# A fused retention and FP4 feed-forward kernel: the set-up reordered, the end written out

## The chip, the cores and the metric

The kernel runs on one NeuronCore of a Trainium2 chip. The metric is the device time of one launch in microseconds, the median of three runs. PE is the matrix engine (TensorE), DVE the vector engine, ACT the scalar engine, POOL GpSimd; SP issues nearly all DMAs. Each engine works through its own instruction list in order, and semaphores are the only thing that ties the lists together.

## The reference

The input x is 8 sequences of 1024 rows of 256 numbers. What is computed, cut to what matters:

```python
xn = layernorm(x)                                   # over the last axis, no gain
# branch 1: retention with 8 heads of 32
Q, K = rotate_and_scale(xn @ W_Q), rotate_and_scale(xn @ W_K, downscale=True)
V = xn @ W_V
scores = (Q @ K^T) * decay_mask                     # causal, gamma_h ** (n - m)
Y = per_head_layernorm(scores @ V) * gn_weight + gn_bias
a = (silu(xn @ W_G) * Y) @ W_O
# branch 2: feed-forward on blockwise FP4 numbers (blocks of 16, scale = max|.|/6)
q = fp4_quant_dequant
h = silu(q(xn) @ q(w_gate)^T) * (q(xn) @ q(w_up)^T)   # 704 wide
f = q(h) @ q(w_down)^T
out = x + a + f
```

## The kernel before

The 8192 rows are 64 tiles of 128 rows (t = 0 to 63; 8 tiles make a sequence). The retention is computed by chunks: within a tile by scores, across tiles by a running 32x32 state for each head, which starts anew with each sequence.

All five engines run a software pipeline that is unrolled in Python. `step(i)` of an engine holds the pieces of several tiles that it does in that step: i+2 (the statistics), i+1 (normalising and quantising x), i (projections, gate and up, rotation, scores), i-1 (values, group norm, quantising h), i-2 (down projection, z), i-3 (the last two matmuls and the residual). So i runs from FIRST = -4 to LAST = 66; steps -2 and -1 fill the pipeline, steps 64 to 66 empty it. The order within a step is written out by hand and is the same in all steps; the pieces that don't exist are skipped.

Products of float32 accuracy are made of three matmuls (`product`, L897 to L900): each operand is split into a high and a low part. A high part is an ACT copy to fp32r, the low part the difference. In step i PE does the product of x with the Q and K columns (`b_qk`, L913), the two transposes of the quantised x (L931), work of older tiles, gate and up in three products (L898 to L900, `gu_c`, `gu_b`, `gu_a`), the V and gate columns (`vg`) and the scores (L1085). The residual (DVE L591) adds x to `b_out` and lets SP store the tile.

The weights are prepared on the chip during the first steps, by pieces that are inserted where `i == -2`, `-1`, `0` or `1`:

- The 1408 gate and up rows come in three parts (n = 0, 1, 2), the down weights in two (n = 3, 4). Each part is quantised: `largest`, `invert`, `divide` (DVE; POOL does `divide` of 3 and 4, L520), `size` (POOL L515, the scale), `magnitude` (ACT L816), `round_off` (DVE, three passes L558, L561, L565; the third waits for `size`).
- Each part is two groups m = 2n, 2n+1. `turn` (PE) transposes a group, `high_part` (ACT L829) copies it, `turn_rest` (PE) forms the remainder in PSUM and `low_part` (ACT L835) copies it; for groups 4 and 5 the low part is DVE's `low_difference`. `double` and `clear_low_half` handle the last 64 rows of the down weights.
- The projection weights `w_qkvg` are two halves, Q and K (c = 0), V and gate (c = 1). `total_qkvg(c)` (ACT L847, four instructions with an accumulator) sums the rows, `mean_qkvg(c)` (POOL L502) scales, `centre_qkvg` subtracts the mean: for c = 0 ACT does it (L854), for c = 1 POOL (L508). Then `turn_qkvg`, `qkvg_high_part` (L861), `turn_qkvg_rest`, `qkvg_low_part` (L868), for m = 0, 1 (c = 0) and m = 2, 3 (c = 1).

In the steps that empty the pipeline, PE keeps the step's order: in step 64 the transposes of z and of h of tile 62 stand before the state and value matmuls of tile 63, and in step 65 the transposes of z of tile 63 (L941, which wait for z) stand before all that is left of tile 63's feed-forward:

```python
pe.wait_ge(z_ready, t + 1)                    # step(i), t = i - 2
... z transposes, h transposes (L946, L950), first down matmuls (L989), rest of them
```

On DVE the sum of squares of tile t (L656) comes after the h remainders of tile t-1 and the first rounding pass (L644) of tile t.

## Time and profile before

| | us |
|---|---|
| median of 3 runs | 898.14 (897.17 to 898.86) |
| the profiled execution, its own time | 897.34 |
| its span in the trace | 895.5 |
| PE busy | 861.6 (96%) |
| DVE busy | 839.4 (94%) |
| POOL busy | 678.7 (76%) |
| ACT busy | 444.5 (50%) |

The span is the time from the first to the last event of the profiled execution; 1.84 us of its own time lie outside it. Busy time is the sum of an engine's instructions, overlaps counted once.

### The profile page before, as it was taken

What the parts mean: (1) busy time and instruction counts of PE and PEld (TensorE: products, weight loads), DVE (VectorE), ACT (ScalarE), POOL (GpSimd) and SP (SyncE); (2) the same over time, 40 slices, a digit from 0 to 9 for tenths busy, and PEclk for the clock granted to TensorE, in tenths of its full rate; (3) what the DMA queues carried; (4) which work ended last, traced back from release to release, by engine and by line L of the source; (5) the groups of instructions that cost most, each with busy time, mean ns of one, the idle gap of its engine ahead of it and who ended that gap; (6) DMA issues with size and microseconds to landing.
All of it is one profiled execution on the core that took longest, in us unless ns stands there. A gap on an engine that the chain in (4) does not pass through costs nothing.

```text
span 895.5 us, 21445 instructions
## 1 busy us (share of the span) xinstructions
PE 861.6 (96%) x8370; PEld 747.2 (83%) x8370; DVE 839.4 (94%) x1883; ACT 444.5 (50%) x1146; POOL 678.7 (76%) x794
## 2 busy tenths in 40 slices
PE   2789999999999999999999999999999999999996
PEld 1668888888888888888888888888888888888885
DVE  7879999999999999999999999999999999999985
ACT  5654454545445454454554445454454544545442
POOL 4767777778778777877877777787787778778774
PEclk9999999999999999999999999999999999999999
DMA  9200110110111011011101101101110110110000
GB/s 322 92 1 19 37 37 19 37 37 24 32 37 33 23 37 37 19 36 37 31 26 36 37 19 37 37 24 31 37 36 20 37 38 18 37 37 13 7 13 18
DMA packets 30052, 33.68 MB, mean 38 GB/s; under 512 B 3328, under 2 KB 28672, under 8 KB 29696
## 3 DMA queue, kind: packets, MB, share of 16 engines
q1 hardware_dynamic: 29808, 32.26, 11.5%
q8 instruction: 66, 1.08, 0.5%
q14 instruction: 34, 0.28, 0.1%
q10 hardware_dynamic: 144, 0.07, 0.0%
HBM read 23.92 MB, written 8.39 MB: 36 GB/s over the span
## 4 chain that ended last, share of the span: by engine, by line
PE 93%; POOL 2%; DVE 2%; ACT 1%; DMA 1%; issue 1%; SPq 0%; POOLq 0%; DVEq 0%
PE quad L900 12%; PE quad L898 12%; PE quad L899 12%; PE quad L1085 5%; PE bank L898 5%; PE quad L966 4%; PE quad L989 4%; PE bank L900 3%; PE bank L899 3%; PE bank L1022 3%; PE quad L1069 3%; PE quad L990 3%; PE quad L946 2%; PE quad L950 2%; PE quad L958 2%; PE quad L1074 2%
## 5 line engine op out<-in xcount | busy, mean ns | idle before, releaser
L898 PE MATMUL quad<-w_gu_hi,xqT_hi 128*128 128x512 f32 (+1 forms) x384 | 149.5, 389 | 1.9 <-DVE xqT_lo L600 1.9
L900 PE MATMUL quad<-w_gu_hi,xqT_lo 128*128 128x512 f32 (+1 forms) x384 | 143.8, 375 | 0.0
L899 PE MATMUL quad<-w_gu_lo,xqT_hi 128*128 128x512 f32 (+1 forms) x384 | 142.5, 371 | 0.0
L467 POOL TENSOR_TENSOR rstd<-var_eps,power 128x9 f32<-128x9 f32 x67 | 124.1, 1852 | 5.6
L456 POOL TENSOR_TENSOR x_quot<-xn,x_inv 128x256 f32<-128x256 f32 x64 | 40.4, 631 | 89.8 <-DVE x_inv L648 89.8
L442 POOL TENSOR_TENSOR h_quot<-h,h_inv 128x704 f32<-128x704 f32 x64 | 88.9, 1390 | 5.1
L475 POOL TENSOR_TENSOR xT_lo<-xT_in,xT_hi 128x256 fp32r<-128x256 f32 x64 | 47.4, 740 | 59.9 <-ACT xT_hi L797 59.9
L452 POOL TENSOR_TENSOR qk<-qk_cos,qk_sin 128x512 f32<-128x512 f32 x64 | 82.9, 1295 | 5.8 <-PE bank L976 0.8
L495 POOL TENSOR_TENSOR gate_gn<-gate,gn 128x512 f32<-128x512 f32 x64 | 82.9, 1296 | 0.0
L900 PEld LDWEIGHTS quad<-w_gu_hi,xqT_lo 128*128 128x128 f32 x384 | 72.0, 188 | 11.4
L898 PEld LDWEIGHTS quad<-w_gu_hi,xqT_hi 128*128 128x128 f32 x384 | 72.5, 189 | 9.7 <-issue 2.0
L899 PEld LDWEIGHTS quad<-w_gu_lo,xqT_hi 128*128 128x128 f32 x384 | 72.7, 189 | 8.5
L807 ACT ACTIVATE xn<-x_in,x_shift,rstd 128x256 f32<-128x256 f32 x64 | 38.5, 602 | 78.8 <-POOL x_shift L479 78.8
L658 DVE SCALAR_TENSOR_TENSOR h_grid<-h_magic,h_diff 128x704 f16<-128x704 bf16 x64 | 76.7, 1198 | 0.0
L729 ACT ACTIVATE xqT_hi<-bank 128x256 fp32r<-128x256 f32 x64 | 24.6, 385 | 97.6 <-PE bank L931 97.6
L465 POOL TENSOR_SCALAR var_eps<-moments 128x9 f32<-128x9 f32 x67 | 60.3, 899 | 7.6 <-DVE moments L656 4.3
L713 DVE TENSOR_TENSOR probs<-quad,causal 128x512 f32<-128x512 f32 x64 | 44.2, 690 | 22.9 <-PE quad L1085 22.2
L778 ACT ACTIVATE silu<-quad 128x512 f32<-128x512 f32 x64 | 38.3, 599 | 51.1 <-PE quad L900 51.1
L761 ACT ACTIVATE x_magic<-x_quot 128x256 bf16<-128x256 f32 x64 | 26.7, 417 | 71.7 <-POOL x_quot L456 71.7
L752 ACT ACTIVATE y_sq<-bank 128x256 f32<-128x256 f32 x64 | 24.6, 384 | 75.1 <-PE bank L1016 75.1
L668 DVE TENSOR_TENSOR hq<-h_grid,h_scale 128x704 f32<-128x704 f16 x64 | 57.8, 904 | 0.1
L898 PE MATMUL bank<-w_qkvg_hi,xT_hi 128*128 128x512 f32 x128 | 57.2, 447 | 0.3 <-POOL xT_lo L475 0.3
(176 smaller groups left out, 2893.2 us busy)
## 6 DMA issues: line engine op xcount, KB each, us to landing
x_in<-in_x_dram SPq DMA_DIRECT2D x64, 128.0 KB, 2.2
xT_in<-in_xT_dram SPq DMA_DIRECT2D x64, 128.0 KB, 2.2
out_dram<-y_out SPq DMA_DIRECT2D x64, 128.0 KB, 1.7
sin<-const_sin_dram SPq DMA_DIRECT2D x1, 1792.0 KB, 11.4
raw<-in_w_gu_dram SPq DMA_DIRECT2D x2, 512.0 KB, 7.2
w_qkvg<-in_w_qkvg_dram SPq DMA_DIRECT2D x1, 1024.0 KB, 8.3
cos<-const_cos_dram SPq DMA_DIRECT2D x1, 896.0 KB, 7.2
raw<-in_w_down_dram SPq DMA_DIRECT2D x2, 352.0 KB, 8.7
```

The lines of the kernel that those rows point to most:

```text
L442: pool.tensor_tensor(blocks(h_quot[:]), blocks(h[:]), spread(h_inv[:]), ALU.mult).then_inc(h_divided, 1)
L452: pool.tensor_tensor(qk[:], qk_cos[:], qk_sin[:], ALU.add).then_inc(rope_add, 1)
L465: pool.tensor_scalar(var_eps[:], moments[:, 1:], EPS, None, ALU.add).then_inc(var_ready, 1)
L467: pool.tensor_tensor(rstd[:, (t + 3) % RING, 0:1 + H], var_eps[:], power[:], ALU.pow).then_inc(rstd_ready, 1)
L475: pool.tensor_tensor(xT_lo[:], xT_in[:, t % SLOTS], xT_hi[:].bitcast(F32), ALU.subtract).then_inc(x_low, 1)
L495: pool.tensor_tensor(gate_gn[:, t % 2, :, :], gate[:].unsqueeze(1).broadcast_to([P, 2, D]), gn[:], ALU.mult).then_inc(gate_scaled, 1)
L658: dve.scalar_tensor_tensor(h_grid[:], h_magic[:], LEAST, h_diff[:], ALU.max, ALU.subtract).then_inc(h_gridded, 1)
L668: dve.tensor_tensor(blocks(hq[:, 0:F]), blocks(h_grid[:]), spread(h_scale[:]), ALU.mult).then_inc(h_quant, 1)
L898: pe.matmul(out, hi[:, k], w_hi[:, k], start=start, stop=False)
L899: pe.matmul(out, hi[:, k], w_lo[:, k], start=False, stop=False)
L900: return pe.matmul(out, lo[:, k], w_hi[:, k], start=False, stop=stop)
L1085: ins = pe.matmul(quad[:, r, g * P:(g + 1) * P], kT[rows, g, :], qT[rows, g, :], start=True, stop=True)
```

## The change

Nothing in the arithmetic changes, and steps 2 to 63 stay as they are but for two leftover pieces of set-up in ACT's step 2. The first part of the diff moves set-up pieces, the second replaces steps 64 to 66 of DVE, ACT and PE by a function `drain()` each, with an order of its own. POOL keeps its steps up to 66. SP is untouched. The core of the diff, condensed to one line for each inserted call, by engine:

```diff
 POOL
 step(-1), before the wait for x_peak:
+    mean_qkvg(0)
 step(0), after the rotation's add (L452):
+    size(4); divide(4)
 step(-1), after x_quot (L456):
-    mean_qkvg(0)
+    size(1); size(2)
 step(-1), after x_shift (L479):
-    size(1)
     mean_qkvg(1); centre_qkvg()
 between step(-1) and step(0):
-    size(2)
     size(3); divide(3)
-    size(4); divide(4)

 DVE
 step(0), after qk_cos (L603):
+    largest(4); invert(4)
     low_difference(4, 5)
 step(1), after qk_cos:
+    round_off(4)
 step(0), before the product with silu (L684):
-    round_off(4)
 step(-1), at its end:
     round_off(1); round_off(2); largest(3); invert(3)
-    largest(4); invert(4)

 ACT
 step(-1), before x_magic (L761):
     magnitude(0)
+    total_qkvg(0)
     high_part(0, 1)
+    centre_qkvg()
     magnitude(1)
-    total_qkvg(0)
 step(-1), before xn (L807):
-    centre_qkvg()
+    qkvg_high_part(0, 1)
     low_part(0, 1)
+    qkvg_low_part(0, 1)
     total_qkvg(1)
+    magnitude(2)
 step(-1), after xn:
-    magnitude(2); qkvg_high_part(0, 1); qkvg_low_part(0, 1)
 between step(-1) and step(0):
     high_part(2, 3)
-    qkvg_high_part(2); low_part(2, 3)
 step(0), after xqT_hi (L729):
+    low_part(2, 3)
     high_part(4, 5)
+    qkvg_high_part(2)
+    magnitude(3)
     qkvg_low_part(2)
-    magnitude(3)
     out_high_parts()
 step(0), before x_magic:              + qkvg_high_part(3)
 step(0), after x_magic:                 magnitude(4)    - qkvg_high_part(3)
 step(0), before gate (L790):            double(3)       - double(4)
 step(0), high_part(6, 7): moved from before xT_hi (L797) to after it
 step(1): high_part(8), low_part(8), high_part(9), low_part(9), clear_low_half()
     stood before xqT_hi, before yT, before kT, and (the last two) before silu;
     now high_part(8) before x_magic, double(4) before silu, low_part(8) after silu,
     high_part(9) before xT_hi, and in step(2), before xqT_hi:
+    low_part(9); clear_low_half()

 PE
 step(0), before the Q and K product:
-    turn(2, 3)
 step(0), after the Q and K product:
-    turn_qkvg(2)
+    turn(2, 3)
 step(0), after the x transposes:
     turn_rest(2, 3); turn(4, 5)
+    turn_qkvg(2)
     turn_qkvg_rest(2)
 step(1): turn(8), turn_rest(8), turn(9), turn_rest(9) stood before and after the
     Q and K product, before gu_c and after the qk transposes; now after gu_b,
     after gu_a, after vg and after the scores

 DVE, ACT and PE, at the end
-for i in range(LAST + 1):
+for i in range(TILES):
     step(i)
+drain()
```

The order of the new `drain()` functions, with t = 63:

```python
# PE: zT_lo matmuls (61) | z transposes (62) | state matmuls (63) | value matmuls (63)
#     | h transposes (62) | y transposes (63) | down_first, down_rest, project_out (62)
pe.wait_ge(h_twice, t + 1)
turn_h(t)
down_first(t)
turn_z(t)
down_rest(t)
project_out(t)
# DVE: masked0 (63), h_inv (63), z low (62), residual(61), h low 0 (62),
#      sum of squares (63), h low 1 (62), h_diff, h_grid, hq (63), y_part (63),
#      residual(62), h low 0, h low 1, z low, residual (63)
# ACT: z high (62), yT (63), h high 0 (62), y_sq (63), h high 1 (62), h_magic (63),
#      last 64 columns of hq (63), h high 0, h high 1, z high (63)
```

The new PE functions issue the same matmuls as the step did. `down_first(t)` waits for the first high part of h and for the residual of tile t-1, then does 6 matmuls; `down_rest(t)` does 11 in the order high part 1, low part 1, low part 0, each behind its wait; `project_out(t)` does 4 with z's high part and 2 with its low part.

## Rows read from the trace of the kernel before

**Rows 1.** The page's chain that ended last, shares of the span by engine.

```profile
PE 93%; POOL 2%; DVE 2%; ACT 1%; DMA 1%; issue 1%; SPq 0%; POOLq 0%; DVEq 0%
```

**Rows 2.** Windows: start:end, length, busy us of each engine, granted PE clock, DMA.

```profile
75.50:858.00 782.50, 782.50 (x7730) 680.62 (x7724) 753.90 (x1723) 390.54 (x1014) 610.04 (x717) 1.00 0.10 30
...
884.00:895.50 11.50, 5.50 (x31) 4.96 (x31) 2.70 (x7) 1.43 (x4) 2.80 (x3) 0.85 0.07 23
```

**Rows 3.** Timeline, set-up, ACT: start, duration, instruction, [idle before, releaser].

```profile
12.65 0.49 ACT L829 ACTIVATE w_gu_hi<-quad 128x384 fp32r<-128x384 f32 x1 [4.03 <-PE quad L1111]
...
14.63 0.41 ACT L847 ACTIVATE w_qkvg<-w_qkvg 128x256 f32<-128x256 f32 x1
...
16.84 1.69 ACT L854 ACTIVATE w_qkvg<-w_qkvg,w_mean 128x256 f32<-128x256 f32 x4
...
41.70 0.60 ACT L868 ACTIVATE w_qkvg_lo<-quad 128x512 fp32r<-128x512 f32 x1 [0.67 <-PE quad L1158]
```

**Rows 4.** SP's issue of the projection weights, and its time to landing.

```profile
3.06 0.43 SPq L401 DMA_DIRECT2D w_qkvg<-in_w_qkvg_dram  x1
...
w_qkvg<-in_w_qkvg_dram SPq DMA_DIRECT2D x1, 1024.0 KB, 8.3
```

**Rows 5.** Timeline, set-up, PE.

```profile
24.08 1.12 PE L1152 MATMUL quad<-ident,w_qkvg 128*128 128x128 f32 x4 [3.53 <-ACT w_qkvg_hi L861]
...
27.71 0.47 PE L898 MATMUL bank<-w_qkvg_hi,xT_hi 128*128 128x512 f32 x1
...
45.45 0.73 PE L1085 MATMUL quad<-qT,kT 32*128 32x128 f32 x16 [0.36 <-ACT val L791]
...
56.02 0.33 PE L1125 MATMUL quad<-ident,raw 128*128 128x128 f32 x1 [1.60 <-ACT w_dn_hi L829]
...
61.70 0.73 PE L1085 MATMUL quad<-qT,kT 32*128 32x128 f32 x16 [1.02 <-ACT val L791]
62.72 0.50 PE L898 MATMUL bank<-w_qkvg_hi,xT_hi 128*128 128x512 f32 x1 [0.29 <-POOL xT_lo L475]
```

**Rows 6.** Timeline, set-up, DVE.

```profile
25.00 1.30 DVE L561 SCALAR_TENSOR_TENSOR w_magic<-w_magic,raw 128x1024 f16<-128x1024 bf16 x1
29.52 1.23 DVE L565 TENSOR_TENSOR raw<-w_magic,w_scale 128x1024 f32<-128x1024 f16 x1 [3.22 <-POOL w_scale L515]
...
32.13 0.88 DVE L540 TENSOR_REDUCE w_max<-raw 128x44 f32<-128x704 f32 x1
```

**Rows 7.** Timeline, set-up, POOL.

```profile
22.56 0.23 POOL L502 TENSOR_SCALAR w_mean<-w_sum 128x4 f32<-128x4 f32 x1
22.89 6.00 POOL L508 TENSOR_SCALAR w_qkvg<-w_qkvg,w_mean 128x256 f32<-128x256 f32 x4
28.97 0.44 POOL L515 TENSOR_SCALAR w_scale<-w_max 128x64 f32<-128x64 f32 x1
...
37.68 1.20 POOL L456 TENSOR_TENSOR x_quot<-xn,x_inv 128x256 f32<-128x256 f32 x1 [0.36 <-DVE x_inv L648]
```

**Rows 8.** Timeline, the end, PE.

```profile
878.64 0.45 PE L958 MATMUL quad<-qT,state 32*32 32x128 f32 x16
...
887.47 0.69 PE L941 MATMUL bank<-ident,z 128*128 128x128 f32 x2 [4.65 <-POOL z L489]
...
892.57 0.40 PE L923 MATMUL quad<-w_out_hi,zT_lo 128*128 128x256 f32 x2
```

**Rows 9.** Timeline, the end, DVE.

```profile
881.64 0.41 DVE L656 TENSOR_REDUCE moments<-y_sq 128x8 f32<-128x256 f32 x1
...
882.88 0.89 DVE L668 TENSOR_TENSOR hq<-h_grid,h_scale 128x704 f32<-128x704 f16 x1
...
893.00 0.42 DVE L591 TENSOR_TENSOR y_out<-quad,x_in 128x256 f32<-128x256 f32 x1 [1.46 <-PE quad L923]
```

**Rows 10.** Timeline, the end, POOL.

```profile
883.05 2.41 POOL L467 TENSOR_TENSOR rstd<-var_eps,power 128x9 f32<-128x9 f32 x1
...
886.69 0.72 POOL L489 TENSOR_TENSOR z<-y_part,gate_gn 128x256 f32<-128x256 f32 x1 [0.54 <-DVE y_part L705]
```

More of the change, by code:

```diff
@@ L452, in step @@
                     pool.tensor_tensor(qk[:], qk_cos[:], qk_sin[:], ALU.add).then_inc(rope_add, 1)
+                    if i == 0:
+                        size(4)
+                        divide(4)
                 if exists(i + 1):
@@ L527, in _ @@
                 step(i)
-            size(2)
             size(3)
             divide(3)
-            size(4)
-            divide(4)
             for i in range(LAST + 1):
@@ L605, in step @@
                     if i == 0:
+                        largest(4)
+                        invert(4)
                         low_difference(4, 5)
+                    if i == 1:
+                        round_off(4)
                 if exists(i + 2):
@@ L695, in step @@
                         invert(3)
-                        largest(4)
-                        invert(4)
                 if exists(i):
@@ L725, in step @@
                     t = i
-                    if i == 1:
-                        high_part(8)
+                    if i == 2:
+                        low_part(9)
+                        clear_low_half()
                     act.wait_ge(x_turned, t + 1)
@@ L889, in _ @@
             high_part(2, 3)
-            qkvg_high_part(2)
-            low_part(2, 3)
-            for i in range(LAST + 1):
+            for i in range(TILES):
                 step(i)
+            drain()
         @block.tensor
@@ L1051, in step @@
                     ins.then_inc(vg_ready, 1)
+                    if i == 1:
+                        turn(9)
                     if i == 0:
@@ new lines, in down_first, with down_rest @@
+            def down_first(t):
+                pe.wait_ge(hT_high0, t + 1)
+                pe.wait_ge(summed, t)
+                for k in range(3):
+                    pe.matmul(b_out, hT_hi[:, k], w_dn_hi[:, k], start=k == 0, stop=False)
+                    ins = pe.matmul(b_out, hT_hi[:, k], w_dn_lo[:, k], start=False, stop=False)
+                ins.then_inc(down_h0, 1)
+            def down_rest(t):
+                pe.wait_ge(hT_high1, t + 1)
+                for k in range(3, 5):
+                    pe.matmul(b_out, hT_hi[:, k], w_dn_hi[:, k], start=False, stop=False)
+                    ins = pe.matmul(b_out, hT_hi[:, k], w_dn_lo[:, k], start=False, stop=False)
+                ins.then_inc(down_h1, 1)
+                pe.wait_ge(hT_low1, t + 1)
+                for k in range(3, 5):
+                    pe.matmul(b_out, hT_lo[:, k], w_dn_hi[:, k], start=False, stop=False)
+                pe.matmul(b_out, hT_hi[:, 5], w_dn_hi[:, 5], start=False, stop=False)
+                pe.matmul(b_out, hT_hi[:, 5], w_dn_lo[:, 5], start=False, stop=False).then_inc(down_l1, 1)
+                pe.wait_ge(hT_low0, t + 1)
+                for k in range(3):
+                    ins = pe.matmul(b_out, hT_lo[:, k], w_dn_hi[:, k], start=False, stop=False)
+                ins.then_inc(down_l0, 1)
@@ new lines, in project_out @@
+            def project_out(t):
+                pe.wait_ge(z_high, t + 1)
+                for k in range(KD):
+                    pe.matmul(b_out, zT_hi[:, k], w_out_hi[:, k], start=False, stop=False)
+                    ins = pe.matmul(b_out, zT_hi[:, k], w_out_lo[:, k], start=False, stop=False)
+                ins.then_inc(out_high, 1)
+                pe.wait_ge(z_low, t + 1)
+                for k in range(KD):
+                    ins = pe.matmul(b_out, zT_lo[:, k], w_out_hi[:, k], start=False, stop=k == KD - 1)
+                ins.then_inc(out_ready, 1)
@@ new lines, in drain @@
+            def drain():
+                t = TILES - 1
+                for k in range(KD):
+                    ins = pe.matmul(b_out, zT_lo[:, k], w_out_hi[:, k], start=False, stop=k == KD - 1)
+                ins.then_inc(out_ready, 1)
+                turn_z(t - 1)
+                pe.wait_ge(masked1, t + 1)
+                for g in range(G):
+                    for r in range(HG):
+                        rows = place(g, r)
+                        ins = pe.matmul(b_yT[g][quarter(r), :], state[rows, g * HD:(g + 1) * HD], qT[rows, g, :], start=True, stop=False)
+                ins.then_inc(st_ready, 1)
+                pe.wait_ge(masked0, t + 1)
+                for g in range(G):
+                    for r in range(HG):
+                        head = (g * HG + r) * HD
+                        ins = pe.matmul(b_yT[g][quarter(r), :], val[:, head:head + HD], probs[:, (r + g) % HG, g * P:(g + 1) * P],
+                                        start=False, stop=True)
+                ins.then_inc(yT_ready, 1)
+                turn_h(t - 1)
+                pe.wait_ge(yT_copy, t + 1)
+                pe.wait_ge(z_low, t)
+                for g in range(G):
+                    ins = pe.transpose(b_y[:, g * P:(g + 1) * P], yT[:, g * P:(g + 1) * P], ident[:])
+                ins.then_inc(y_ready, 1)
+                down_first(t - 1)
+                down_rest(t - 1)
+                project_out(t - 1)
+                pe.wait_ge(h_twice, t + 1)
+                turn_h(t)
[3 more added lines that the diff above has]
+                project_out(t)
@@ L1168, in _ @@
             turn_qkvg_rest(0, 1)
-            for i in range(LAST + 1):
+            for i in range(TILES):
                 step(i)
+            drain()
 AHEAD = 7
```

122 lines of the change are left out of this document (98 added, 24 removed).

## The prediction, made before the changed kernel was run

> **What bounds the kernel now.** I read the page's chain of waits first: 93% of it is PE [rows 1]. Then the windows: from 75.5 to 858 us PE is busy in every microsecond, at the full granted clock [rows 2], DVE in 753.90 of 782.50. The change leaves that stretch alone, so it passes through as it is, and only its ends can move. Its length is 61 to 62 tiles of some 13.1 us, from the scores of tile 1 at 61.70 [rows 5] on. What precedes 61.70, and what follows the last tile's scores, is set by waits; there I went through the timeline engine by engine. A landmark that comes d us earlier at the front is d us at the end, as long as PE stays the bound between.
>
> **The front: the first projection.** ACT now sums the columns before the first high parts. The weights are issued at 3.06 and land 8.3 us later, at 11.4 [rows 4]; four sums at 0.40 us each (14.63 to 16.23 before, [rows 3]) end at 13.0. The high part that was ready at 12.65 so starts 0.35 us late, a loss that I count: it is what the transposes behind it wait for. The centring stood at 16.84 and took 1.69 us [rows 3]; now it runs at 13.8 to 15.5, directly behind the high parts. PE's transposes of these weights start near 15.7. Their high parts no longer stand behind the second half's sums, xn and magnitude(2), but behind magnitude(1), x_magic and xT_hi (1.05 + 0.4 + 0.4, to 17.0), so the remainder group that started at 24.08 can start at 17.6, 6.5 us earlier. It took 3.6 us from there to the Q and K product at 27.71 [rows 5]; the product comes at 21.2. This large shift is not the gain, since what it needs next is elsewhere: PE goes on to wait for the second weight part.
>
> **The front: DVE and POOL.** DVE stood 3.22 us before its third rounding pass because POOL gave the scale of part 2 only at 28.97, behind its 6.00 us of centring [rows 6, 7]. Now POOL makes both scales near 15.3 to 16.3. What is late next is magnitude(2): ACT does it after the sums of the second half, 21.15 + 1.6 + 1.0 = 23.75. Part 2 is then rounded in 3.75 us, to 27.55; before, to 30.75 (29.52 + 1.23, [rows 6]). DVE also loses largest(4) and invert(4) there (0.88, [rows 6], plus 0.65 for the two small ones) and comes to the work of step 0 some 4.5 us earlier, at 29.1. They come back behind qk_cos.
>
> POOL is the engine that does not get earlier. Its centring needs the sums of the second half, which ACT now ends at 22.75 instead of 20.8; mean and start of centring are 22.8 and 23.15, against 22.56 and 22.89 [rows 7]. The four instructions took 6.00 us. The first took 2.79 of it and the last two 0.92 each, once DVE was idle, so the work alone is 3.7 us and the rest is time lost beside DVE's rounding. In the 3.4 us in which DVE was busy beside it (to 26.30, [rows 6]), about 1.1 us of work got done. With the same rate beside the 3.75 us of rounding part 2, the centring ends at 29.6. From below 28.0 (a full 3.7 us of work plus 1.2 lost), from above 30.5. From 29.6 POOL does, without a wait: size(3), divide(3), x_scale, the rotation's add, size(4), divide(4), by 35.1, and x_quot of tile 1 in 1.20 us, as at 37.68 [rows 7], since DVE is in the same rounding pass then. It ends at 36.3 against 38.88, 2.6 us earlier.
>
> The Trainium skill, SBUF — State Buffer, section "Who interferes with whom", says that a DVE instruction with two SBUF inputs and a GpSimd instruction that reads SBUF exclude each other for a whole instruction. The stretched 2.79 us in the trace agree in kind. By the strict rule the second centring instruction would wait out all the rounding: 27.55 + 2.8 = 30.35, so 0.75 us less gain.
>
> **The front: steps 0 and 1.** Behind x_quot stand on ACT x_magic, magnitude(4), the two copies of k and q, and the last low part of the projection weights, which ran at 41.70 [rows 3] and now ends at 38.6 instead of 42.3. PE has finished its third gate-up product by then (at 38.3) and starts the V and gate columns at 38.65. The scores of tile 0, waiting for val, start at 40.9 against 45.45 [rows 5]: 4.5 us earlier. Now xT_hi of tile 1 goes ahead of the high parts 6 and 7, so POOL's xT_lo no longer holds the next product up, and turn(8), which stood in front of it, is gone from there: the Q and K product of tile 1 comes at 43.05, not 48.17, 5.1 us earlier. In step 1 PE lost 1.60 us to the high part of group 9 [rows 5]; its transposes now stand behind vg, at the price of a wait of about 0.3 us for the low part of group 8, and round_off(4), three passes of 0.9, is on DVE before h_diff. I find the scores of tile 1 at 56.05 (61.70 before). The last remainder, group 9, then stands between the scores and the next product, and high_part(9) ahead of xT_hi: tile 2's product at 57.4 against 62.72 [rows 5]. The front gains **5.2 us**. Its bounds: 3.3 if the centring and ACT's chain are each a microsecond later than drawn and step 1's last insertions cost their full 0.8 us of PE; 6.4 if the centring ends at 28.0.
>
> **The end** (in the times of before, without the front's shift). Before, the state matmuls of tile 63 start at 878.64, behind six transposes of h of tile 62 that wait for the masked scores [rows 8]. Now they come first, some 1.2 us earlier, the y transposes and y_sq 1.0 us earlier, and on DVE the sum of squares stands ahead of h_diff: it starts at 880.05, not 881.64 [rows 9], 1.6 us earlier. POOL's eps and power (2.41, [rows 10]) and all behind it move with it, so z is ready at 885.8, not 887.4. The quantised h of tile 63 (882.88 + 0.89, [rows 9]) stays where it was, for h_magic is behind one more copy.
>
> Before, PE sat idle for 4.65 us until z, and had then everything of tile 63 to do: 5.5 us from 887.47 to the end of the last matmul (892.57 + 0.40, [rows 8]). Now the h transposes run at 884.2, down_first at 885.4 (it waits for the residual of tile 62, 885.35), and z's transposes at 886.1; left are 17 matmuls 0.12 us apart and the last one's 0.16: 888.55. The old last matmul ended at 892.97, so the gain is 4.4. This holds at the full clock. In the last window of before the granted clock is 0.85 [rows 2], so part of it ran at the lower of its levels, 1.2 GHz, right behind the 4.65 us of idleness. The new order leaves PE idle for only 1.35 us (882.85 to 884.2). If the clock falls anyway, the first 12 instructions take 1.0 us longer and the gain is 3.4. I take 4.2; the bounds are 2.9 and 4.8.
>
> The Trainium skill, TensorE: Matmul & The Clock Gate, section "What's actually happening", says that an idle array runs at half clock until activity releases it. The trace agrees where the idleness was 4.65 us; whether 1.35 us is enough for it no row here shows.
>
> **Sum.** 5.2 + 4.2 = 9.4 us off 897.34, the profiled execution's own time: 887.9. The median of the runs is 0.8 above that execution: 888.7.
>
> **Rivals.**
> 1. *POOL's centring is stretched further* and carries the whole of step 0. For it: 2.79 us for a 0.92 us instruction, beside the very kind of pass that will run beside it now. Against it: two of four ran free. It gives a front gain of 3.3 and the same end: 890.6. Chance 0.17.
> 2. *The clock falls in the short gap, and the end gains only its first part.* For it: the 0.85 of [rows 2]. Against: the gap is under a third of the old one. 888.7 + 1.2 = 889.9. Chance 0.17.
> 3. *The front gain is given back in step 2*, because the last low part and clear_low_half (0.8 us of ACT) now stand ahead of xqT_hi, and ACT's early arrival is eaten by a DVE that is behind; only the end counts: 898.14 - 4.2 = 893.9. Against it: ACT is idle half of the time. Chance 0.04.
> 4. *Slower.* The steady stretch settles into another phase of DVE against POOL, in which their shared passes collide more. DVE has (782.50 - 753.90) / 60 = 0.48 us to spare for each tile [rows 2]; beyond that it sets the pace. It decides from 0.48 + 9.4 / 61 = 0.63 us of added stretch for each tile; at 0.7 us the kernel takes 888.7 + 61 x 0.22 = 902. For it: DVE's passes do get stretched. Against: PE's own order sets the phase and is unchanged. Chance 0.03.
> 5. *The moves do nothing at the front*, the total being set by a landing. Against it: DMA is idle in the stretch from 30 us on, and every landing needed precedes that. The end alone, as in 3: 893.9. Chance 0.03.
>
> **How the numbers follow.** The forecast has 0.56. A measurement can tell 0.2%, 1.8 us. Faster needs under 896.3, which all cases but the fourth and a remnant give: 0.94; within 0.2%, 0.03; slower, 0.03. Bounds of both terms, 3.3 + 2.9 and 6.4 + 4.8, give 892.0 and 886.9, and a run's median may lie 0.7 to either side: the range is 886.2 to 892.7.
>
> **What would show it.** Right: column sums starting at 11.4; the Q and K product of tile 0 near 21; no wait of DVE for the scale, but a short one for magnitude(2); centring ending at 29 to 30; scores of tiles 0 and 1 at 41 and 56; PE without idle time until the end; from the last state matmuls to the last residual's start 11.2 us (877.4 to 888.6) instead of 14.4 (878.64 to 893.00). Wrong: idle PE in step 2 or later, centring past 31, or z's transposes later than 887.

## The result, and the profile of the changed kernel

| | before | after |
|---|---|---|
| median of the runs | 898.34 us (897.17 to 898.86, 5 runs, the three of the earlier table among them) | 888.18 us (887.87 to 889.64, 5 runs) |
| profiled execution | 897.34 us, span 895.5 | 888.04 us, span 886.2 |

The ratio is 0.9895 [0.9881, 0.9908]. The forecast was 888.7 for the median and 9.4 us off the profiled execution's time; that one moved by 897.34 - 888.04 = 9.30 us. The five runs of the changed kernel lie in two groups, 887.87, 888.04, 888.18 and 889.41, 889.64; that comes back below.

First the chain of waits of the changed kernel: PE's share is what it was in [rows 1], and POOL's has gone from 2% to 1% while DVE's rose from 2% to 4%.

```profile
PE 93%; DVE 4%; POOL 1%; DMA 1%; issue 0%; ACT 0%; SPq 0%; POOLq 0%
```

Windows of the changed kernel, in the columns of [rows 2]. The long stretch is PE's alone as before. The last stretch is the first difference: its granted clock is 1.00, where [rows 2] had 0.85.

```profile
50.00:53.00 3.00, 3.00 (x16) 2.41 (x16) 3.00 (x9) 1.17 (x4) 1.49 (x2) 1.00 0.02 5
70.00:852.00 782.00, 782.00 (x7727) 680.27 (x7727) 753.35 (x1723) 389.54 (x1011) 609.35 (x717) 1.00 0.10 30
878.00:886.20 8.20, 4.10 (x31) 3.66 (x31) 3.76 (x8) 1.51 (x4) 0.94 (x2) 1.00 0.09 32
```

The set-up, PE. The landmarks of [rows 5] have moved: the remainder group 24.08 to 17.55, the Q and K product of tile 0 27.71 to 20.99, the scores of tile 0 45.45 to 40.62, the product of tile 1 48.17 to 42.39, the scores of tile 1 61.70 to 56.28, the product of tile 2 62.72 to 57.57. Among the waits that are left are 1.07 us for DVE's rounding, 0.59 for the centring, and in step 1 a new one of 1.69 for POOL's qk.

```profile
17.55 0.66 PE L1316 MATMUL quad<-ident,w_qkvg 128*128 128x128 f32 x4 [0.45 <-ACT w_qkvg_hi L943]
...
20.99 0.47 PE L979 MATMUL bank<-w_qkvg_hi,xT_hi 128*128 128x512 f32 x1 [1.86 <-POOL xT_lo L481]
...
27.21 0.66 PE L1275 MATMUL quad<-ident,raw 128*128 128x128 f32 x4 [1.07 <-DVE raw L567]
...
28.90 0.71 PE L1303 MATMUL quad<-by_head,w_qkvg 128*128 128x128 f32 x4 [0.59 <-POOL w_qkvg L513]
...
40.62 0.73 PE L1163 MATMUL quad<-qT,kT 32*128 32x128 f32 x16 [0.36 <-ACT val L844]
...
42.39 0.40 PE L979 MATMUL bank<-w_qkvg_hi,xT_hi 128*128 128x512 f32 x1
...
49.31 0.66 PE L1096 MATMUL bank<-ident,qk 128*128 128x128 f32 x4 [1.69 <-POOL qk L454]
...
56.28 0.73 PE L1163 MATMUL quad<-qT,kT 32*128 32x128 f32 x16 [0.80 <-ACT val L844]
...
57.57 0.50 PE L979 MATMUL bank<-w_qkvg_hi,xT_hi 128*128 128x512 f32 x1
```

ACT in the set-up, against [rows 3]: the column sums begin as soon as the weights land, and the centring follows the first high parts directly.

```profile
10.41 0.42 ACT L929 ACTIVATE w_qkvg<-w_qkvg 128x256 f32<-128x256 f32 x1 [1.71 <-DMA w_qkvg<-in_w_qkvg_dram]
...
12.74 0.49 ACT L911 ACTIVATE w_gu_hi<-quad 128x384 fp32r<-128x384 f32 x1 [0.62 <-PE quad L1275]
...
13.77 1.69 ACT L936 ACTIVATE w_qkvg<-w_qkvg,w_mean 128x256 f32<-128x256 f32 x4
```

DVE in the set-up, against [rows 6]: the third rounding pass of part 1 stands at 21.96, that of part 2, which had 3.22 us of waiting, at 25.77, both without a wait, and part 2 is rounded at 25.77 + 1.38 = 27.15. The last two rows are one pass of the same size: 0.89 us in step 0, 1.83 in step 1.

```profile
21.96 1.22 DVE L567 TENSOR_TENSOR raw<-w_magic,w_scale 128x1024 f32<-128x1024 f16 x1
...
25.77 1.38 DVE L567 TENSOR_TENSOR raw<-w_magic,w_scale 128x1024 f32<-128x1024 f16 x1
...
36.51 0.89 DVE L567 TENSOR_TENSOR raw<-w_magic,w_scale 128x704 f32<-128x704 f16 x1
...
48.17 1.83 DVE L567 TENSOR_TENSOR raw<-w_magic,w_scale 128x704 f32<-128x704 f16 x1
```

POOL in the set-up, against [rows 7]: the centring ends at 23.38 + 5.47 = 28.85, x_quot of tile 1 at 35.72 instead of 38.88. No row has a wait, and several durations are long: POOL works without a break and is stretched.

```profile
16.80 2.74 POOL L473 TENSOR_TENSOR rstd<-var_eps,power 128x9 f32<-128x9 f32 x1
...
22.02 1.26 POOL L507 TENSOR_SCALAR w_mean<-w_sum 128x4 f32<-128x4 f32 x1
23.38 5.47 POOL L513 TENSOR_SCALAR w_qkvg<-w_qkvg,w_mean 128x256 f32<-128x256 f32 x4
...
34.52 1.20 POOL L461 TENSOR_TENSOR x_quot<-xn,x_inv 128x256 f32<-128x256 f32 x1
...
46.44 0.91 POOL L448 TENSOR_SCALAR x_scale<-x_max 128x16 f32<-128x16 f32 x1
47.43 1.83 POOL L454 TENSOR_TENSOR qk<-qk_cos,qk_sin 128x512 f32<-128x512 f32 x1
```

The end, PE, against [rows 8], from the scores of tile 63. The idle stretch is 1.42 us where it was 4.65, it stands ahead of the transposes of h and no longer ahead of those of z, and these are now surrounded by work.

```profile
870.53 0.73 PE L1163 MATMUL quad<-qT,kT 32*128 32x128 f32 x16
...
872.07 0.45 PE L1229 MATMUL quad<-qT,state 32*32 32x128 f32 x16 [0.16 <-DVE probs L715]
...
879.31 0.55 PE L1178 MATMUL quad<-ident,hq 128*128 128x128 f32 x3 [1.42 <-ACT hq L891]
...
880.44 0.39 PE L1188 MATMUL quad<-w_dn_hi,hT_hi 128*128 128x256 f32 x1 [0.25 <-ACT hT_hi L873]
...
881.25 0.38 PE L1173 MATMUL bank<-ident,z 128*128 128x128 f32 x2
```

DVE in the end, against [rows 9]: the sum of squares, the quantised h, the last residual.

```profile
874.83 0.41 DVE L748 TENSOR_REDUCE moments<-y_sq 128x8 f32<-128x256 f32 x1
...
877.78 1.19 DVE L755 TENSOR_TENSOR hq<-h_grid,h_scale 128x704 f32<-128x704 f16 x1
...
883.70 0.42 DVE L720 TENSOR_TENSOR y_out<-quad,x_in 128x256 f32<-128x256 f32 x1 [1.19 <-PE quad L1216]
```

POOL in the end, against [rows 10]: the power starts at 875.66 and takes 1.83 us, not 2.41, and then z.

```profile
879.38 0.72 POOL L494 TENSOR_TENSOR z<-y_part,gate_gn 128x256 f32<-128x256 f32 x1 [1.16 <-DVE y_part L757]
```

I measure each end of the kernel from one landmark, the scores of tile 63. PE's row of them in the kernel before:

```profile
875.70 0.73 PE L1085 MATMUL quad<-qT,kT 32*128 32x128 f32 x16
```

They were at 875.70 and are at 870.53, so the front gave 5.17 us. From them to the start of the last residual it was 893.00 - 875.70 = 17.30 us and is 883.70 - 870.53 = 13.17: the end gave 4.13.

### The profile page after: what moved, and what is told of

Read it like the earlier page. It is cut to its first block, busy times and chain, and to the rows that moved or that the text cites. A ratio compares the mean times of both kernels' runs of the same rounds, so it can differ in the third digit from the quotient of the medians.

```text
span 886.2 us, 21445 instructions
## 1 busy us (share of the span) xinstructions
PE 859.9 (97%) x8370; PEld 744.5 (84%) x8370; DVE 840.4 (95%) x1883; ACT 443.7 (50%) x1146; POOL 679.7 (77%) x794
## 4 chain that ended last, share of the span: by engine, by line
PE 93%; DVE 4%; POOL 1%; DMA 1%; issue 0%; ACT 0%; SPq 0%; POOLq 0%
PE quad L981 12%; PE quad L979 12%; PE quad L980 12%; PE bank L979 5%; PE quad L1163 5%; PE quad L1042 4%; PE quad L1065 4%; PE bank L981 3%; PE bank L980 3%; PE bank L1096 3%; PE quad L1147 3%; PE quad L1066 2%; PE quad L1034 2%; PE quad L1022 2%; PE quad L1026 2%; PE quad L1152 2%
## 5 line engine op out<-in xcount | busy, mean ns | idle before, releaser
L981 PEld LDWEIGHTS quad<-w_gu_hi,xqT_lo 128*128 128x128 f32 x384 | 72.0, 188 | 11.4
```

The lines of the kernel that those rows point to most:

```text
L981: return pe.matmul(out, lo[:, k], w_hi[:, k], start=False, stop=stop)
```

## The experiments

Each is compared with the kernel before, run beside it on the same chip: its median was 897.75 for e1 to e4, 897.85 for e5 to e8, 899.12 for e9 to e12. The number in a label is that of its running order. A profile shows one run of each kernel; for e2, e3, e6, e7, e8 and e9 that was the longest one. The diffs are against the changed kernel where nothing else is said.

**The two ends by themselves (e1, e2).** One kernel has the new set-up and the old end (loops to LAST + 1, no drain), the other the old set-up and the new end.

```diff
# e1_front, on DVE, ACT and PE
-            for i in range(TILES):
+            for i in range(LAST + 1):
                 step(i)
-            drain()
# e2_end: the kernel before, with the new loops and drain() of all engines
```

> The set-up of the changed kernel with the old steps 64 to 66 at the end. Theory A (the two ends are separate and add): span shorter than before by what the scores of tile 63 moved, 5.2 us, so 893.1 us for the median; PE idle 4.65 us before z's transposes, granted clock below 1 behind it. Rival B (the front's gain is given back in the steady stretch, the end brought nearly all): 897 to 898.

Measured: 892.2 us (892.0 to 892.47), 5.55 below its before; ratio 0.9937 [0.9922, 0.9951]. The scores of tile 0 are at 40.43, of tile 1 at 56.12. (The projection weights landed 8.6 us after their issue here, not 7.3, ACT's sums began at 11.62 and the first high part behind them at 13.24, half a microsecond later than in the changed kernel, and yet these scores are not later; the rest of the set-up started 0.19 us earlier here.) Its last stretch is that of the kernel before, with the same 4.65 us and the fallen clock. First PE's row of it, then the window.

```profile
882.15 0.69 PE L1015 MATMUL bank<-ident,z 128*128 128x128 f32 x2 [4.65 <-POOL z L494]
```

```profile
880.00:890.20 10.20, 5.46 (x31) 4.92 (x31) 2.70 (x7) 1.37 (x3) 1.47 (x3) 0.83 0.08 26
```

> The old set-up with the new end alone. Theory A: 4.1 us off the median of before, 894.2; scores of tile 1 at 61.7 as before; last residual 13.2 us after the first scores of tile 63. Rival B: 889 to 890, nearly the whole gain.

Measured: 893.24 (893.07 to 894.02), 4.5 below; ratio 0.995 [0.9935, 0.9964]. From the scores of tile 63 (876.51) to the last residual (889.68) it is 13.17 us, exactly as in the changed kernel, and the clock is 1.00 from 880 us on. (In this profile everything starts 0.84 us later, the first high part at 13.49 for 12.65 in [rows 3], hence 876.51 and not 875.70.) 5.55 + 4.5 = 10.05, and both together measured 898.34 - 888.18 = 10.16. The ends add. Nothing of the front is given back in the long stretch.

**The sums back behind the high parts (e3).**

```diff
                         magnitude(0)
-                        total_qkvg(0)
                         high_part(0, 1)
+                        total_qkvg(0)
                         centre_qkvg()
```

> The changed kernel with ACT's first column sums put back behind the first high parts; the centring still stands right behind them. Theory A (POOL's centring of the second half carries step 0, and it starts when ACT has summed the second half): sums end at 15.4 instead of 12.1, ACT's chain is 1.9 to 2.1 us later, so POOL's centring starts 1.5 to 2 us later and the scores of tile 0 at 42.2 to 42.6 (40.6 in the changed kernel): 1.5 to 2.0 us slower than the changed kernel, 889.8. Rival C (the chain has slack there, since the first product waits 1.9 us for POOL's low part of x, not for the weights): less than 0.4 us lost.

Measured: 889.98 (889.33 to 890.01), ratio 0.991 [0.9895, 0.9925]. The product is at 23.14 instead of 20.99, 2.15 us later, the scores of tile 0 at 42.55 and of tile 1 at 58.23, 1.9 us later each. This one swap carries 1.9 of the front's 5.2 us. The size is theory A's, but not its carrier: POOL's centring ends 1.5 us later, at 30.36, and POOL then waits for DVE three times (0.29 us for the inverse of the weights, 0.22 for qk_cos, 0.15 for x_inv), while DVE itself had waited 1.43 us for ACT's magnitude(2).

**The transposes of the second part back ahead of the projection (e4, e9).**

```diff
+                    if i == 0:
+                        turn(2, 3)
                     if t == 0:
...
-                    if i == 0:
-                        turn(2, 3)
```

> The changed kernel with PE's transposes of the second part put back ahead of the first Q and K product. Theory A (DVE reads that product only at 28.9, PE idles before the third part's transposes): the product starts near 24.2 instead of 21.0 and nothing behind 28 us moves, scores of tile 0 at 40.6, no difference in time. Rival D (what the product delays on PE, the transposes of x and the remainders of the second part, comes 1.4 us later and carries on): 0.5 to 1.4 us slower.

Measured: 889.24 (888.79 to 889.81), ratio 0.9905 [0.9888, 0.9921]; the scores of tile 0 at 41.59, 1.0 us late, those of tile 1 at 57.27. The loss has the size that rival D expected, but not its cause. PE's rows of this kernel: after the idle 4.12 us the transposes take 1.11 us (0.66 in the changed kernel) and the products stand 0.43 us apart and not 0.23.

```profile
23.18 1.11 PE L1275 MATMUL quad<-ident,raw 128*128 128x128 f32 x4 [4.12 <-DVE raw L567]
...
24.80 0.78 PE L979 MATMUL bank<-w_qkvg_hi,xT_hi 128*128 128x512 f32 x1
```

The window over them gives the reason, a granted clock of 0.50, the lower of the two levels.

```profile
23.00:28.50 5.50, 5.33 (x19) 4.64 (x20) 5.36 (x8) 1.53 (x3) 5.40 (x5) 0.50 0.57 204
```

To part the order from the clock, the same order once more with 34 transposes of the identity into a free bank, to keep PE busy in the gap.

```diff
# on top of e4_turn
                     if i == 0:
+                        for k in range(34):
+                            pe.transpose(bank[1][:, 0:P], ident[:], ident[:])
                         turn(2, 3)
```

> The kernel e4_turn (second part's transposes back ahead of the first Q and K product) with 34 needless transposes of the identity put into PE's 4.1 us of idleness ahead of them; nothing else is changed. Theory K (e4_turn is a microsecond slower only because the granted clock fell to 0.50 behind that idleness): the clock stays 1.00 from 23 to 28.5 us, the product's six matmuls stand 0.23 us apart, scores of tile 0 at 40.6 to 40.8, time 888.0 to 888.3, as the changed kernel. Rival D (the order itself costs it, the transposes of x come behind the product): scores of tile 0 stay at 41.4 or later, 889 or more.

Measured: 889.24 (888.02 to 891.52), ratio 0.9898 [0.9879, 0.9917]. By the times theory K is not borne out: the median is that of e4, and one run of four lies in the 888.0 to 888.3 that it asked for. The profile, which is of the longest run, parts the two. The product starts late, but runs at the upper clock, and the scores of tile 0 are at 40.68, as in the changed kernel (40.62): up to there the whole microsecond was the clock, and the order itself costs nothing.

```profile
24.16 0.48 PE L979 MATMUL bank<-w_qkvg_hi,xT_hi 128*128 128x512 f32 x1
```

Its windows show where this run lost its time. From 50 us on, in step 1, where nothing differs from the changed kernel, the clock was 0.50, and the scores of tile 1 came at 57.94, 1.7 us late. It was 0.72 in the end too, from 880 to 886, with the same drain.

```profile
23.00:28.50 5.50, 5.07 (x34) 4.21 (x34) 5.38 (x6) 3.18 (x7) 5.40 (x5) 1.00 0.61 196
50.00:53.00 3.00, 3.00 (x10) 2.31 (x9) 2.94 (x8) 0.00 (x0) 1.42 (x2) 0.50 0.00 0
```

PE's rows of that end: the same 1.42 us of idleness as in the changed kernel, the first transposes and matmul as fast as there, and then the matmuls 0.21 us apart. From the scores of tile 63 (872.22) to the last residual (886.90) it is 14.68 us, 1.5 more than in the changed kernel's profile.

```profile
881.00 0.55 PE L1180 MATMUL quad<-ident,hq 128*128 128x128 f32 x3 [1.42 <-ACT hq L891]
...
882.68 0.41 PE L1191 MATMUL quad<-w_dn_lo,hT_hi 128*128 128x256 f32 x1
882.89 0.41 PE L1190 MATMUL quad<-w_dn_hi,hT_hi 128*128 128x256 f32 x1
```

**Who carries step 0, POOL or DVE (e5).** ACT, idle there, takes two of POOL's four centrings.

```diff
-                for j in range(4, 8):
+                for j in range(6, 8):
...
+            def centre_second():
+                act.wait_ge(qkvg_mean, 2)
+                for j in range(4, 6):
+                    act.activation(w_qkvg[:, j, :], w_qkvg[:, j, :], ACT.Identity, bias=w_mean[:, j:j + 1],
+                                   scale=1.0).then_inc(qkvg_centred[1], 1)
```

> The changed kernel with two of POOL's four centring instructions of the second half given to ACT (behind xn, before the second part's high parts). Forecast's theory P (POOL's centring carries step 0): it ends at 26 to 26.5 instead of 28.85, x_quot of tile 1 at about 32.5 instead of 34.52 and the scores of tile 0 1 us or more earlier. Rival theory V (DVE's own list carries it, with no idle time from 19 to 34.5 us; POOL merely arrives at the same time): x_quot moves only by what POOL's stretching of DVE's rounding costs, 0 to 0.4 us, and the scores of tile 0 by 0 to 0.4; time 887.8 to 888.2.

Measured: 887.5 (887.4 to 889.0), ratio 0.9888 [0.9872, 0.9905]. POOL's rows of this kernel: the centring is over at 26.38, 2.5 us earlier, and POOL then waits 1.51 us for DVE's largest.

```profile
23.23 3.15 POOL L513 TENSOR_SCALAR w_qkvg<-w_qkvg,w_mean 128x256 f32<-128x256 f32 x2
27.89 0.39 POOL L520 TENSOR_SCALAR w_scale<-w_max 128x44 f32<-128x44 f32 x1 [1.51 <-DVE w_max L542]
...
33.90 1.20 POOL L461 TENSOR_TENSOR x_quot<-xn,x_inv 128x256 f32<-128x256 f32 x1
```

x_quot ends at 35.10 (35.72), the scores of tile 0 are at 40.00 (40.62), of tile 1 at 55.68 (56.28). So 2.5 us less on POOL is worth 0.6 us at most: 0.15 of it is there before the change acts (the Q and K product at 20.84 for 20.99), and the other 0.46 is one small instruction of DVE, the second w_inv, which took 0.65 us beside POOL's rotation add and takes 0.19 now. That is nearer to theory V (0 to 0.4) than to P (1 us or more): DVE carries step 0, and POOL's part in it is what it stretches on DVE. My prediction had named POOL the carrier.

**Step 1: two passes of the last rounding moved out of it (e6),** to the end of step 0, where DVE was idle. `round_first` holds the first two of the three passes, `round_last` the third.

```diff
                     if i == 1:
-                        round_off(4)
+                        round_last(4)
...
+                    if t == 0:
+                        round_first(4)
```

> The changed kernel with the first two passes of DVE's rounding of part 4 moved from step 1 to the end of step 0, where DVE stands idle for 1.48 us; the third pass stays. Theory R (in step 1 the rounding stretches POOL's x_scale and rotation add, 0.91 and 1.83 us instead of 0.27 and 1.28, and PE waits 1.69 us for it): PE's wait falls to 0.3 to 0.8, scores of tile 1 at 55.0 to 55.5 (56.28 in the changed kernel), 887.1 to 887.5. Rival T (POOL is late because h_quot starts late, and DVE is busy anyway): the wait stays above 1.3 and the time at 888.2 or, since the two passes delay x_max, up to 0.5 slower.

Measured: 890.26 (889.32 to 890.75), ratio 0.9912 [0.9898, 0.9927], and the scores of tile 1 at 59.05, 2.8 us late. Both theories fall. The 1.69 us for qk did go, but only because PE comes later still: POOL's add now takes 1.27 us and not 1.83, and ends at 50.82, where it had ended at 49.26. DVE's rows show what took the place of that wait: beside POOL's gate_gn and the low part of the output weights the two passes take 1.89 and 1.84 us, not 0.87 and 0.89, x_max starts at 45.80 and not 43.64, and PE waits 2.67 us for probs, with a granted clock of 0.50 from 47 to 53 behind it. What the late passes and what the clock cost of the 2.8 us is not parted by a run. DVE's rows, then POOL's add:

```profile
42.11 1.89 DVE L573 SCALAR_TENSOR_TENSOR raw<-w_magic,raw 128x704 f32<-128x704 bf16 x1
44.03 1.84 DVE L576 SCALAR_TENSOR_TENSOR w_magic<-w_magic,raw 128x704 f16<-128x704 bf16 x1
45.80 0.41 DVE L596 TENSOR_REDUCE x_max<-xn 128x16 f32<-128x256 f32 x1
```

```profile
49.55 1.27 POOL L454 TENSOR_TENSOR qk<-qk_cos,qk_sin 128x512 f32<-128x512 f32 x1
```

**The sum of squares back behind h_diff (e7),** as in the kernel before, the rest of the drain left.

```diff
-                dve.wait_ge(squared, t + 1)
-                dve.tensor_reduce(moments[:, 2:], ...)
                 h_low_part1(t - 1)
                 dve.wait_ge(h_abs, t + 1)
                 dve.scalar_tensor_tensor(h_diff[:], ...)
+                dve.wait_ge(squared, t + 1)
+                dve.tensor_reduce(moments[:, 2:], ...)
```

> The changed kernel with the sum of squares of the last tile put back behind h_diff in the written-out end. Forecast's theory Z (z's path sets the end, 1.6 us of its gain come from this move): z's transposes and the last residual 1.2 us later, 889.4. Rival H (the end now hangs on the quantised h: its transposes, high part and first down matmuls; z has 1.1 us to spare): less than 0.5 us, z's transposes at most 0.3 later, 888.2 to 888.7.

Measured: 892.13 (891.25 to 893.66), ratio 0.9936 [0.9921, 0.9951]; from the scores of tile 63 to the last residual 17.26 us and not 13.17. Both expectations are far too small. The profile is of the longest of the four runs and had lost 1.5 us in step 1 as well; by the medians the move back costs 892.13 - 888.18 = 3.95 us, by the fastest runs 3.4. PE's rows, then DVE's:

```profile
880.62 0.55 PE L1178 MATMUL quad<-ident,hq 128*128 128x128 f32 x3 [1.34 <-ACT hq L891]
...
883.60 0.55 PE L1188 MATMUL quad<-w_dn_hi,hT_hi 128*128 128x256 f32 x1 [2.10 <-DVE y_out L720]
```

```profile
882.70 0.42 DVE L757 TENSOR_TENSOR y_part<-bank,y_gain 128x256 f32<-128x256 f32 x1 [2.42 <-POOL y_gain L477]
883.04 0.41 DVE L720 TENSOR_TENSOR y_out<-quad,x_in 128x256 f32<-128x256 f32 x1
```

The down product accumulates where the residual of tile 62 has to be read first, and that residual stands on DVE behind y_part, which waits 2.42 us for POOL's gain. So all of PE's last work waits for z's path, not only the transposes of z. It starts 11.58 us behind the scores of tile 63 and not 9.91, which is 1.67 of the 4.1 us. The other 2.4 come behind it: the matmuls stand 0.21 us apart, 0.12 in the changed kernel, at a granted clock of 0.71 from 880 to 891.8.

**What the clock is worth in the old end (e8):** the kernel before, with 36 transposes of the identity ahead of its wait for z.

```diff
# against the kernel before
                     t = i - 2
+                    if i == TILES + 1:
+                        for k in range(36):
+                            pe.transpose(bank[1][:, 0:P], ident[:], ident[:])
                     pe.wait_ge(z_ready, t + 1)
```

> The kernel before, with 36 needless transposes of the identity into an unused bank put into PE's 4.65 us of idleness ahead of the last tile's z transposes; nothing else is changed. Theory K (the lower clock behind the idleness costs over 1 us): the granted clock stays 1.00 in the last 11 us, the last six h transposes take 0.49 instead of 0.85 for three, last residual 1.0 to 1.3 us after less time: 896.5 to 896.9 against 897.8. Rival L (the ACT copies between set the pace): less than 0.4 us.

Measured: 896.53 (896.29 to 899.39, 10 runs), 1.3 below its before by the medians; ratio 0.9991 [0.9982, 1.0001], which leaves the total open. Three of the ten runs are 1.7 us or more above the median, and the profile is of the longest. Its scores of tile 1 are at 63.64 and not 61.70, 1.6 us of that lost in step 1 with a granted clock of 0.57 from 56 to 60 us, and 3.57 us lie between the start of the last residual and the end of the span, for 2.50. The end between these is clearer, 16.47 us from the scores of tile 63 to the last residual instead of 17.30, with a granted clock of 1.00 in the stretch of the gap (0.87 in the kernel before). The 0.83 us gained lie between theory K (1.0 to 1.3) and rival L (under 0.4), nearer to K.

```profile
56.00:60.00 4.00, 3.65 (x11) 2.97 (x12) 1.96 (x5) 1.65 (x6) 2.91 (x3) 0.57 0.00 0
...
880.00:890.00 10.00, 9.28 (x105) 8.48 (x104) 5.21 (x11) 2.77 (x7) 5.90 (x5) 1.00 0.07 24
```

**The two groups of runs (e10).** Two runs of the changed kernel are 1.5 us longer; their mean granted clock is 0.998 against 1.000. The falls seen in the kernel with filled order, whose mean is 0.996, are candidates, 1.5 to 1.7 us each. Ahead of the one in step 1 PE is idle for 1.69 us, so 12 transposes of the identity were put there.

```diff
                     t = i
+                    if i == 1:
+                        for k in range(12):
+                            pe.transpose(bank[6][:, 0:P], ident[:], ident[:])
                     pe.wait_ge(rope_add, t + 1)
```

> The changed kernel with 12 needless transposes of the identity into an unused bank, put ahead of PE's wait for the rotated q and k in step 1, where it is idle for 1.7 us. Theory M (the runs fall into two groups 1.5 us apart, 887.9 to 888.2 and 889.4 to 889.6, because in some of them the granted clock falls to half in step 1 behind 44 to 50 us with PE busy only half of the time): the upper group disappears or becomes rarer, all runs within 887.7 to 888.4. Rival N (the spread has another source, the landing of the first weights for instance): the spread stays 1.5 us.

Measured: 888.8, from 887.91, 888.04, 889.56, 889.57; ratio 0.989 [0.9875, 0.9905]. The two groups are still there, though the idle time ahead of that wait is down to 0.38 us: theory M fails as it was put. The profile was of a run of the lower group (scores of tile 1 at 56.17), so it isn't shown whether the clock fell in step 1 of the longer ones all the same or somewhere else, and the mean clock doesn't settle it (one run of the lower group, 888.04, has 0.998 too). What the profiles of other kernels show: three that are of their kernel's longest run (e7, e8, e9) had all lost some 1.6 us between the scores of tiles 0 and 1 (a fourth, e2, had started late), and with the drain of the changed kernel the clock fell in the end once in nine profiles (e9).

**The best of it together (e11, e12),** ACT's share of the centring with the 12 transposes, and in a second kernel the quantised h of tile 63 also earlier in the drain.

```diff
# e12_end2 against e11_both: DVE, and the same on ACT with h_magic and h_high_part1
-                h_low_part1(t - 1)
                 dve.wait_ge(h_abs, t + 1)
                 dve.scalar_tensor_tensor(h_diff[:], ...)
+                h_low_part1(t - 1)
```

> The changed kernel with the shared centring of e5_share and the 12 transposes of e10_fill1. If both act: 887.3 to 887.7 and no run above 888.2. If the fill has no effect: as e5_share, 887.4 with single runs at 889.0.

> e11_both with an end in which ACT's h_magic of the last tile stands ahead of the second high part of tile 62, and DVE's h_diff ahead of the second low parts. Theory H (the end hangs on the quantised h, from h_magic on): hq ends 0.4 to 0.5 us earlier, but PE's work of tile 62 ends 0.2 to 0.4 us later and becomes the next wait: 0.1 to 0.4 us less, 887.0 to 887.4. Rival Z (the end hangs on z and on the residual of tile 62): no change against e11_both.

Measured: 887.87 (887.37 to 888.84), ratio 0.9881 [0.9866, 0.9896], and 887.51 (887.27 to 887.85), ratio 0.9876 [0.9859, 0.9892]. The first is above the 887.3 to 887.7 that both parts acting would give, and one of its four runs is above 888.2, so no effect of the 12 transposes is shown. The end of the second is 13.06 us against 13.17: moving h forward is worth 0.1, since PE's work for tile 62 (waits of 0.52 and 0.59 in it) is the next to be late. The second has the lowest ratio of all, but the changed kernel's 0.9895 [0.9881, 0.9908] was measured at another time and the intervals overlap; that it beats the changed kernel is not shown.

## Why the prediction was right, step by step

**The sum** holds, and each half: front 5.17 us for 5.2, end 4.13 for 4.2. Both kernels with one end each confirm it apart from the profile. That it holds to 0.1 us is in part luck: within the front errors of up to a microsecond cancel, within the end ones of 0.2 to 0.4, as follows.

**First projection: right, with small errors that cancel.** I had the sums at 11.4; the weights landed 7.3 us after their issue, not 8.3 as in [rows 4], and the sums stand at 10.41. They end before the first high part can start, so the 0.35 us that I charged was not paid. In the kernel with the new set-up alone it was, and more (the high part at 13.24), and the scores of tile 0 came no later: the term costs nothing either way, since PE's next wait is for POOL. The remainder group came at 17.55 (17.6), the product at 20.99 (21.2). What I hadn't seen is that PE then waits 1.86 us for POOL's xT_lo: the groups ahead ran faster than in [rows 5], where the four transposes took 1.12 us (the pace of the lower clock, see the end of this document), and POOL was slower. The sums ahead of the high parts are worth 1.9 us, measured alone.

**POOL's centring: the number near by two errors, the role wrong.** I drew it from 23.15 to 29.6. ACT's sums of the second half ended at 21.35, 1.4 us earlier than drawn, but POOL started the centring only at 23.38, since its power took 2.74 us and the mean 1.26 (0.23 in [rows 7]), both beside DVE's rounding. The centring itself took 5.47 us for my 6.45. The step that failed is "POOL is the engine that does not get earlier", as the carrier of step 0: DVE has no listed wait from 16 to 38 us, not even the short one for magnitude(2) that I had announced, and taking 2.5 us off POOL gave 0.6 at most. DVE's own 3.22 us of waiting were gone, as the prediction had it, and DVE's sequence then came out at what I had drawn for POOL's: x_quot ended at 35.72 (36.3).

The Trainium skill, SBUF — State Buffer, "Who interferes with whom", by whose strict rule I had the centring end at 30.35 (an estimate; with the rounding's measured end of 27.15 it is 29.95), is not borne out in that strictness: it ended at 28.85, and both sides paid: POOL took 5.47 us for work that alone takes 3.7, and DVE's last rounding pass beside it 1.38 us, for 1.22 one part earlier.

**Steps 0 and 1: right at both ends, wrong between.** Step 0 was 0.3 to 0.7 us better than drawn (scores 40.62 for 40.9, product of tile 1 at 42.39 for 43.05), step 1 a microsecond worse: 56.28 - 42.39 = 13.9 us where I had 13.0. The missing microsecond is PE's 1.69 us for qk. I had put round_off(4) on DVE into step 1 at "three passes of 0.9"; one took 1.83 us, and beside them POOL's size went to 0.91 and the rotation's add to 1.83 (1.28 in step 0). The term was mis-sized on POOL's side, the one that I didn't count. The next theory, that these passes only need a free place, fell too: in an idle place of DVE they cost 2.8 us. The clock's fall is part of these 2.8. That the passes and what POOL does beside them stretch each other is what both profiles show.

**The end: right, and for a better reason than mine.** The state matmuls came 2.94 - 1.54 = 1.40 us earlier after the scores (1.2), and from there to the last residual it is 11.63 us (11.2, before 14.36). The sum of squares stands 4.30 us behind the scores (4.35), z is ready at 9.57 (10.1), the h transposes stand at 8.78 (8.5), since the quantised h was stretched to 1.19 us. I had split the end into 1.6 us of earlier z and some 2.8 of work moved into the gap. The run that undoes the first alone gives back 4.1 in its profile and 3.4 to 4.0 in the times, more than twice 1.6, so in the time they are not separate terms: without the earlier sum of squares the residual of tile 62, which I had named as what down_first waits for, holds all of the work that was to fill the gap, and the clock falls on top. By the path alone, with the clock's 2.4 us taken off, the loss is 1.67 us, which is the size that I had given it, through another wait; that the clock hangs on the same move I had not seen. I had the residual's time and didn't ask what stood ahead of it.

**The clock at the end.** PE idles for 1.42 us (1.35 forecast), and the granted clock stays at 1.00 in the changed kernel's profile, as in that of the old set-up with the new end. It is not certain to: with the same drain and gap it fell in the profile of the filled order, one of nine. In the old end the gap was 4.65 us and the clock fell; filling it shortened the end by 0.83 us, where I had 1.0. The Trainium skill, TensorE: Matmul & The Clock Gate, "What's actually happening", says that an idle array runs at half clock until activity releases it. The 0.50 behind 4.12 us of idle PE in the set-up agrees.

**The rivals.** POOL's further stretch: there was more of it, but ahead of the centring, and it didn't set the time. The clock in the short gap: it stayed in this profile, and the forecast of 1.0 us for its fall was too small where it happened (1.5). The front's gain lost in step 2, and the landing-bound front: 5.17 us are still there at tile 63, and ACT's new work in step 2 delayed nothing (product of tile 2 at 57.57 for 57.4). The steady stretch in another phase: PE is busy in each of 782.00 us.

**Left open:** where the upper group of runs loses its 1.5 us, in step 1, in the end or elsewhere. If it is the fall in the end, the second rival is what these executions do.

## What to carry to other kernels

Where the middle is PE without a gap, take the two ends apart with one landmark each (the first and the last tile's scores) and add; here that held to 0.1 us. When a stalled engine's wait is removed, draw the next engine's timeline to its end before naming the carrier, and count a pass of DVE beside POOL on both sides: here one went from 0.89 to 1.83 us and POOL's add beside it from 1.28 to 1.83. In a drain, ask of each wait on a queue what stands ahead of the instruction that releases it: a residual of one tile behind a factor of the next was worth some 4 us, 2.4 of it by the lower clock behind the wait.

## What the runs showed of the hardware that was not expected

The same instructions in step 1 ran at a granted clock of 1.00 in the changed kernel (50 to 53 us), at 0.53 in the kernel with the late sum of squares and at 0.50 in the one with filled order, though nothing in this stretch differs between them; it costs some 1.5 us (scores of tile 1 at 57.79 and 57.94 for 56.28). It is not a matter of the new set-up: the old one had 0.57 there in the profile of e8. Ahead of it PE was idle for 1.69 us in the changed kernel and 1.71 in the one with filled order. In the end it was 1.42 us in both of these, and the clock fell in one (14.68 us for 13.17). The length of the gap alone doesn't decide it.

The column of the granted clock has to be read together with the rows. From 23 to 28.5 us it says 1.00 for the kernel before and 0.50 for the same code in e8, but four transposes take 1.12 us in both, which is what they take at 0.50 in e4 (1.11); in the changed kernel they take 0.66. So [rows 5] were in part rows of the lower clock, though the column didn't say so.

DVE and POOL stretch each other in both directions and by different factors. POOL's size of 16 columns took 0.27 or 0.91 us, its power of 9 columns 1.83, 2.41 or 2.74, and DVE's 704-wide rounding passes from 0.87 to 1.89, the longest each beside work of the other.

The transfer of the 1 MB of projection weights landed 8.3 us after its issue in the kernel before, 7.3 in the changed one and 8.6 in the one with the new set-up alone, as much of a difference as several of the steps that I had worked out to a tenth. Here no effect on the scores of tile 0 is seen (40.62 with 7.3, 40.43 with 8.6).
